# A residual is turned token-major by DMA and VectorE block turns in place of TensorE transposes

## The reference

```python
lam = sigmoid(x @ W.T + b)                        # W 2048 x 2048
s_t = lam_t * s_(t-1) + (1 - lam_t) * x_t         # a scan along the sequence
x = layernorm(x + s)
logits = x @ router_weight.T                      # 8 experts, top 2, softmax of the two
shared = (g * sigmoid(g) * u) @ sh_down.T         # g = x @ sh_gate.T, u = x @ sh_up.T, inner size 8192
routed = (same form, inner size 1024) * comb_w    # comb_w: sum of the two softmax weights
x = layernorm(x + shared + routed)
```

## Time and profile before

| | |
|---|---|
| Median of 3 runs | 1680.43 us (1680.02 to 1680.74) |
| The profiled execution's own time | 1681.68 us |
| Its span, slowest core (core 0) | 1680.1 us |
| Spans of the 8 cores | 1676.4 to 1680.1 us |
| Mean granted clock of the cores | 0.994 to 0.998 |
| TensorE busy | 1637.7 us (97%) |
| VectorE, ScalarE, GpSimd busy | 397.8, 209.0, 255.9 us |

### The profile page before, as it was taken

One profiled execution on the slowest core, in us unless ns is written; L12 is line 12 of the kernel. 1 busy time (PEld: TensorE's weight loads), 2 busy tenths in 40 slices (PEclk: granted clock), 3 DMA queues, 4 the chain that ended last, 5 costly groups with the idle time before them and its releaser, 6 DMA issues.

```text
span 1680.1 us, 19416 instructions; the slowest of 8 cores (1676.4 to 1680.1 us)
## 1 busy us (share of the span) xinstructions
PE 1637.7 (97%) x7788; PEld 761.8 (45%) x7945; DVE 397.8 (24%) x580; ACT 209.0 (12%) x330; POOL 255.9 (15%) x365
## 2 busy tenths in 40 slices
PE   5999999999999999999999999999999999999997
PEld 2544444444444444444444444444444444555443
DVE  0579610122011122000122011122000121011276
ACT  3354410000000000000000000000000000122011
POOL 5878420011010011010011010011010011000000
PEclk8999999999999999999999999999999999999999
DMA  9936094069442068451078461178460179525222
GB/s 195 200 62 113 14 142 69 1 101 153 76 80 43 6 109 141 75 90 34 10 116 131 78 96 22 20 121 128 76 102 7 23 123 144 94 36 99 38 101 101
DMA packets 43047, 141.44 MB, mean 84 GB/s; under 512 B 5064, under 2 KB 6864, under 8 KB 42960
## 3 DMA queue, kind: packets, MB, share of 16 engines
q0 software_dynamic: 38768, 126.94, 47.1%
q1 hardware_dynamic: 2464, 8.93, 1.7%
q10 hardware_dynamic: 1728, 4.33, 0.7%
HBM read 253.45 MB, written 8.39 MB: 156 GB/s over the span
## 4 chain that ended last, share of the span: by engine, by line
PE 93%; DVE 2%; DMA 2%; issue 2%; POOL 1%; ACT 0%; DVEq 0%; POOLq 0%; ACTq 0%
PE PS L187 92%; DMA wat<-wa 2%; DVE PS L232 1%; PE PS L548 1%; POOL accq L272 0%; POOL accs L269 0%; POOL xfA L158 0%; DVE xfA L353 0%; DVE accs L269 0%; DVE xfA L355 0%; POOL wat L152 0%; DVE xfB L240 0%; POOL step L217 0%; ACT ot L642 0%; ACT PS L223 0%
## 5 line engine op out<-in xcount | busy, mean ns | idle before, releaser
L187 PE MATMUL PS<-xbA,gu 128*128 128x512 bf16 x2255 | 505.1, 379 | 2.6
L187 PE MATMUL PS<-xbB,gu 128*128 128x512 bf16 x2257 | 504.8, 379 | 2.5
L187 PE MATMUL PS<-y,dw 128*128 128x512 bf16 x1882 | 413.2, 379 | 2.1
L187 PEld LDWEIGHTS PS<-xbA,gu 128*128 128x128 bf16 x2304 | 225.3, 98 | 270.4 <-issue 0.6
L187 PEld LDWEIGHTS PS<-xbB,gu 128*128 128x128 bf16 x2304 | 225.5, 98 | 269.4
L187 PEld LDWEIGHTS PS<-y,dw 128*128 128x128 bf16 x1920 | 187.9, 98 | 226.5
L454 DVE TENSOR_TENSOR y<-silu,PS 128x512 bf16<-128x512 f32 x128 | 88.0, 688 | 762.8 <-PE PS L187 722.8
L449 ACT ACTIVATE silu<-PS 128x512 f32<-128x512 f32 x144 | 85.9, 597 | 1218.3 <-PE PS L187 1103.8
L514 POOL DMA_DIRECT2D dw<-wd x80 | 42.4, 536 | 644.3 <-PE PS L187 639.4
L374 POOL DMA_DIRECT2D gu<-wg x72 | 39.1, 543 | 409.1 <-PE PS L187 395.3
L187 PE MATMUL PS<-xbA,wat 128*128 128x512 bf16 (+1 forms) x502 | 77.1, 314 | 24.1 <-DMA wat<-wa 18.3
(11 more groups left out here) (85 smaller groups left out, 459.9 us busy)
## 6 DMA issues: line engine op xcount, KB each, us to landing
gu<-wg POOLq DMA_DIRECT2D x72, 512.0 KB, 6.7
gu<-wu POOLq DMA_DIRECT2D x72, 512.0 KB, 8.4
dw<-wd POOLq DMA_DIRECT2D x80, 384.0 KB, 7.2
wat<-wa POOLq DMA_DIRECT2D x13, 512.0 KB, 52.5
wl<-wl POOLq DMA_DIRECT2D x12, 512.0 KB, 5.8
xfA<-xa POOLq DMA_DIRECT2D x7, 641.0 KB, 16.5
xfB<-xb SPq DMA_DIRECT2D x8, 513.0 KB, 14.4
out_own<-ot SPq DMA_DIRECT2D x8, 512.0 KB, 3.1
```

The costliest lines, as they stand in the source:

```text
L187: return P.op("PE", lambda: nc.tensor.matmul(out, lhs, rhs, start=start, stop=stop), after=after, tok=tok)
```

## The change

The TensorE transposes and their ScalarE copies are replaced. `move(m)` (m = 0 to 15: a pair of chunks k, k + 1 of the half h = m % 2) issues 16 DMAs from SP, SBUF to SBUF. Each takes the 32 partitions of quarter a and the columns of quarter b of both chunks to the partitions of quarter b, into the first 128 columns of a chunk of `xfA` (the earlier tokens, not used any more). There is room for two moves. Then `turn(m)` on VectorE turns each 32 x 32 block, 128 x 512 at once, one instruction for each of the two chunks, back to the residual's place. `move(0)` and `move(1)` are issued behind k = 1 of the last down pass; in strips c = 1 to 8 each `gate_up` is followed by `turn(m)` and `move(m + 2)`. A token tile then holds 32 tokens out of each 128 of its half and no longer 128 adjacent ones, so in the last pass y is written in the matching order, and the host reorders the output rows.

```diff
             y = yt[s % SPP][:, h * 512:(h + 1) * 512]
+            up, sl, cw = bank(bu), silu[i][:, :], comb[:, h * 512:(h + 1) * 512]
+            if s >= (NPASS - 1) * SPP:
+                y = y.rearrange("p (n b i) -> p b n i", n=4, b=4)
+                up, sl, cw = (v.rearrange("p (b n i) -> p b n i", n=4, b=4) for v in (up, sl, cw))
             if s < NSH:
-                t_u = P.op("DVE", lambda: nc.vector.tensor_tensor(y, silu[i][:, :], bank(bu), op=ALU.mult),
+                t_u = P.op("DVE", lambda: nc.vector.tensor_tensor(y, sl, up, op=ALU.mult),
...
-        def turn(k, h, b):
-
-            x = own(k, h)
-            for j in range(4):
-                t = P.op("PE", lambda j=j: nc.tensor.transpose(bank(b, 128, j * 128), x[:, j * 128:(j + 1) * 128],
-                                                               ident[:, :]),
-                         after=[t_r2[k, h], t_const, bank_free[b]], tok=(j == 3))
-            bank_free[b] = t_tm[k, h] = P.op("ACT", lambda: nc.scalar.copy(x, bank(b)), after=[t])
+        xw = xfA.ap().rearrange("p (g m q c) -> p g m q c", g=2, m=2, c=XA)
+        xv = (xva[:, :, 1 + WARM:], xvb[:, :, 1:])
+        t_mv = {}
+        mv_busy = [None] * 2
+
+        def move(m):
+
+            k, h = m // 2 * 2, m % 2
+            x = xv[h]
+            for a in range(4):
+                for b in range(4):
+                    dst = xw[32 * b:32 * b + 32, m % 2, :, a, 0:128]
+                    t = P.dma("SP", f"cMV{m % 2}", lambda dst=dst, a=a, b=b: nc.sync.dma_start(
+                        out=dst, in_=x[32 * a:32 * a + 32, k:k + 2, 128 * b:128 * b + 128]),
+                        after=[t_r2[k + 1, h], mv_busy[m % 2]])
+            t_mv[m] = t
+
+        def turn(m):
+
+            for j in range(2):
+                k, h = m // 2 * 2 + j, m % 2
+                x = own(k, h).rearrange("p (n a j) -> p a n j", n=4, a=4)
+                src = xw[:, m % 2, j, :, 0:128].rearrange("p a (n i) -> p a n i", n=4)
+                mv_busy[m % 2] = t_tm[k, h] = P.op("DVE", lambda x=x, src=src: nc.vector.transpose(x, src),
+                                                   after=[t_mv[m]])
...
+                if last and k == 1:
+                    move(0)
+                    move(1)
...
-                    if last and 2 <= c < 10:
-                        for j in range(2):
-                            turn(2 * (c - 2) + j, h, 6 + j)
+                    if last and 1 <= c < 9:
+                        m = 2 * (c - 1) + h
+                        turn(m)
+                        if m + 2 < ND:
+                            move(m + 2)
```

More of the change, by code:

```diff
@@ L459, in gate_up @@
                            after=[t_s, t[1]])
-                t_y[s, h] = P.op("DVE", lambda: nc.vector.tensor_tensor(
-                    y, silu[i][:, :], comb[:, h * 512:(h + 1) * 512], op=ALU.mult), after=[t_u, t_comb[0]])
+                t_y[s, h] = P.op("DVE", lambda: nc.vector.tensor_tensor(y, sl, cw, op=ALU.mult),
+                                 after=[t_u, t_comb[0]])
             bank_free[bu] = t_u
@@ L611, in build_program @@
         t_out = []
-        xv = (xva[:, :, 1 + WARM:], xvb[:, :, 1:])
         for n in range(8):
@@ L739 @@
         bi, hi = c // 2, c % 2
-        out[bi, hi * TPC:(hi + 1) * TPC, :] = res.results[c]["out_own"]
+        o = res.results[c]["out_own"].reshape(2, 4, 4, 32, D).transpose(0, 2, 1, 3, 4)
+        out[bi, hi * TPC:(hi + 1) * TPC, :] = o.reshape(TPC, D)
     return out
```

## The result

The changed kernel takes 1702.2 us (median of 4 runs, 1700.6 to 1702.8) against 1680.2 for the kernel before: ratio 1.0129, 95% interval 1.0112 to 1.0147. It is slower by 22 us, where 14 less were forecast.

A forecast was written before the change was run, and what follows sets the result against it. The prediction took TensorE to bound the kernel: removed transposes give back 13.9 us and the added work is hidden at 0, so the profiled span falls from 1680.1 to 1666.2 us. Forecast 1666.5 us, range 1664.8 to 1671.5.

The forecast's parts named there:

- What bounds the kernel: Whole kernel: TensorE sets the time, busy 97% of the span, with 93% of the chain of work that ended last.
- the removed work: Last pass's strip loop: 16 blocks of TensorE transposes at 0.87 us go, giving back 13.9 us, all on the path.
- VectorE's part: Strip loop: 32 added turns of 0.7 us, 1.4 us a slot, hidden beside TensorE; y's new order costs 0.
- Added on SP: SP's queue, last pass: 256 transfers, 0.45 us an issue, 7.2 us a move against 6.91 a slot; 0 on the path.
- lateness formula: Strip loop: turn m's lateness from issue time and landing, largest at m = 15: 1.4 + 224u + L - 103.7 us.
- The bounds, 5.4 to 7.7 us: SP's queue: cost of a move's 16 issues, at 0.34 to 0.48 us each.
- a rival of 0.07: SP's queue: issues slower, 0.76 us as in POOL's three-dimensional load; 50 us late on TensorE, 1717 us; chance 0.07.
- the 21 us of slack: Strip loop: a turn may start about 21 us late before TensorE waits for a bank of the ring of six.
- u: SP's queue: time of one issue in us, taken as 0.45.
- The DMA engines' part: Last pass: a move takes 1.8 to 3.2 us on every engine, 0.3 of a slot taken; fits beside the weights.
- The rival of a slipping cycle: Strip loop: turn, issue and landing slip behind weight loads; 9 us on TensorE, 1675.4 us if every move; chance 0.10.
- Transfers one after another: SP's moves: each transfer begins only when the one before has landed, 28.8 us a move, 1946 us; chance 0.02.

The follow-up runs named there:

- no_turn: The changed kernel without moves and turns, the residual left channel-major and its output term wrong: 1666.0 us, ratio 0.9917 to the kernel before.
- The two lighter doses: only14 and only12: the changed kernel with 14 or 12 of the 16 transfers in moves 2 to 15: 1686.2 and 1667.2 us.
- pool_half: The changed kernel with the same 256 transfers, half of them issued from POOL's queue instead of SP's: 1666.5 us, ratio 0.9921 to the kernel before.
- spread: The changed kernel with turns 0 to 3 moved into the last down product and the others one to a strip: 1665.7 us, ratio 0.9918.
- four: The changed kernel with four chunks in a transfer, 128 issues of 64 KB, one move under way, a turn every third step: 1665.4 us, ratio 0.9912.
- forms: The kernel before with nine groups of dummy transfers of different shapes issued from SP in an idle stretch: 1679.4 us.
- only14: The changed kernel with 14 of 16 transfers in moves 2 to 15: 1686.2 us, ratio 1.0040 to the kernel before.
- only12: The changed kernel with 12 of 16 transfers in moves 2 to 15: 1667.2 us, ratio 0.9924 to the kernel before.

## Why the prediction was wrong

**What bounds the kernel; the removed work.** Right: in no_turn the loop is 13.9 us shorter on every core, as summed, and the whole time 13.6 (1679.6 to 1666.0).

**VectorE's part.** Right: 0.7 us a turn was taken, 0.69 measured, hidden. The rule on the transposing front end (the Trainium skill, "Vector Engine (DVE) Microarchitecture Reference", section 3.8), one element per cycle and lane, is borne out in this: the turn costs what a product of the size costs, 0.69 us.

**Added on SP.** Here is the failed step: the price of an issue, "I take 0.45, 7.2 us a move: the back-to-back case is the nearer one." It was 0.60, 0.64 from start to start, and 0.70 in the mean of the fourteen moves with the long ones, 11.2 us a move. By the lateness formula, as an estimate, issues of 0.64 alone would have cost TensorE about 22 us, more than the gain; the long ones, whose cause is open, made that 35. The bounds, 5.4 to 7.7 us, were drawn from loads of constants and from stores with long rows, none of which is a copy from SBUF to SBUF with 512 B runs; the upper one was no bound. The row of POOL's three-dimensional load, 0.76 us, was the nearest in form and was given to a rival of 0.07 with "SP's own stores took 0.34 at most". That rival was right in its mechanism and place, but 0.76 was no measure of this form either (POOL's own issue of it took 0.54), and its 1717 us came out 15 too high. The estimate from the Trainium skill's "DMA: Bandwidth & Descriptors" (512 cycles on earlier generations, 0.43 us) is too low as well; the runs decide for 0.585 to 0.60.

**The lateness formula** was right. With the measured 11.2 us a move and a last landing of 2 us: 1.4 + 14 x 11.2 + 2 - 103.7 = 56.5 us late. Turn 15 began at 1584.8 and was due at 1403.4 + 18 x 6.91 + 0.96 = 1528.8: 56.0 late, 35 on TensorE with the 21 us of slack. The turn that held TensorE last was the one before it, since move 14 landed late, 4.4 us after its last issue ended (1573.2 to 1577.6). Turn 14 began at 1577.7, due 1521.9, 55.8 late. The up product behind it began at 1579.71 in place of 1403.43 + 20.5 x 6.91 = 1545.1, 34.6 late. The slack was thus 21.2 us, as predicted. The two lighter doses agree with it. "TensorE begins to wait at u = 0.535, and the gain is used up at u = 0.60" was right for an even u.

**The clock** was not in the sum. Behind the first stalls it need not be: SP sets the pace, so what TensorE loses by a lower clock it no longer waits for at the next late turn. Behind the last stall no wait is left to take it up: 34.6 us late at 1579.71, and 2.7 more in the half step at the lower clock (6.11 in place of 3.45 from start to start), make the 37.3.

**The DMA engines' part.** Right in size. In the kernel after, from 1460 to 1600 us, SP's transfers have 17.6% of 16 engines for 14720 packets: 27 ns a packet, in the bounds of 22 and 50. The landing had 3.2 us as median where 3.5 was taken; single ones took 10.6, with weight loads on the engines (82% of them from 1506 to 1516 us). Move 8 landed that way at 1516.0, 10 us behind its last issue, and so the idle of 12.59 us is larger than its neighbours. SP's queue lost nothing by it, since move 9's issues ran meanwhile (1506.1 to 1517.2). The rival of a slipping cycle, with its load pair in the way, thus describes single turns and not the pace: pool_half and spread, with weight loads beside them and longer landings, have no idle.

**"Transfers one after another"** was rightly held small: landings of 1.8 us and more overlap at issues 0.64 apart. The advice of the Trainium skill, "DMA: Bandwidth & Descriptors", to merge transfers under 64 KB is borne out by four, though not for its fixed time of some 2 us. Such a time is there (in forms a transfer of 16 KB landed after 1.8 us and one of 64 KB after 2.1), but it overlaps; what merging saved is the issuing queue's time.

## What to carry to other kernels

A transfer has three prices: bytes on the DMA engines, time to landing, and the time of the queue that issues it. Count the third as instructions by the row of the same form, source and destination included; if no row has that form, the cheapest rows near it are no upper bound. Work that is off the critical path needs a rate as well as a total: with n transfers for each slot of the bounding engine, queue time must be under the slot, or lateness grows linearly and eats the buffers' slack, after which it costs one for one. Here three edits cure it and turn 22 us of loss into 13 to 14.5 us of gain: half of the issues on another idle queue, half as many larger transfers, or an earlier start at an even pace. A queue whose engine takes part in the loop is no idle queue.

## What the runs showed of the hardware beyond that

SP's issue of a transfer took 0.32 us for whole 4 KB rows to or from memory, 0.55 for [32, 2, 128] with memory at one end, 0.49 to 0.54 for 4 KB rows within SBUF, and 0.59 to 0.62 for 512 B runs within SBUF, whether of 16, 32, 64 or 128 KB. POOL's took 0.54 for the same move. TensorE ran the half step behind idles of 12.59, 6.97 and 6.42 us in 6.35, 6.11 and 5.98 us in place of 3.6 (granted clock 0.51 over the first such stretch), and behind shorter idles at times no slower (3.61 behind 1.83 us, and 3.61 behind 2.87 in only14) and at times partly (5.22 behind 2.56 in only12).
